# Trainium2 kernel of four conv layers: longer loops, loads on two queues, paired stores, and a bank of sums copied by two engines

## The reference

```python
# layer 0 runs on a group-normed x, layer 1 on x + layer 0
def _gn(v, G=8, eps=1e-5):          # mean and variance over 2 channels x 128 x 128
    ...
# layer 1: a global mean and max of the normed map, two gates from them
out1 = jnp.mean(x, axis=(2, 3), keepdims=True)
out3 = jnp.max(x, axis=(2, 3), keepdims=True)
wh_weight = jax.nn.sigmoid(jnp.tanh(conv1x1(conv1x1(x, Wc, bc) / (out1 + EPS), W2, b2)))
gray_weight = jax.nn.sigmoid(jnp.tanh(conv1x1(conv1x1(x, W1, b1) / (out3 + EPS), W3, b3)))
out = conv1x1(x * (1.0 + wh_weight + gray_weight), W4, b4)
# layer 2: rational functions of the 9 neighbours, summed
pw = wins[..., None] ** jnp.arange(DEG_P)                 # powers 0 to 5
P = jnp.einsum('pbchwi,fcpi->fpbchw', pw, A)
Q = 1.0 + jnp.abs(jnp.einsum('pbchwi,fcpi->fpbchw', pw[..., 1:5], Bc))
out = jnp.sum(P / Q, axis=(1, 3))
```

## Time and profile before

| | us |
|---|---|
| median of 3 runs | 9667.91 |
| lowest and highest run | 9665.2, 9704.05 |
| the profiled execution | 9659.51 |
| its span | 9657.6 |

### The profile page before, as it was taken

The page is one execution under the profiler, slowest core; times in us unless marked ns, Lnnn a source line. Parts: engine busy times, 40 slices in busy tenths (PEclk is TensorE's granted clock), DMA queues, the critical chain, the costliest instruction groups (busy, mean ns, idle before and its releaser), DMA issues. The chain is left out here.

```text
span 9657.6 us, 141494 instructions
## 1 busy us (share of the span) xinstructions
PE 8079.0 (84%) x35042; PEld 2745.1 (28%) x35042; DVE 7784.3 (81%) x9341; ACT 7530.9 (78%) x8315; POOL 6169.8 (64%) x3354
## 2 busy tenths in 40 slices
PE   5999999999999999402998999899899899992799
PEld 2333333333333333100222222222222222220233
DVE  6777777777777776775999999899899999894787
ACT  4666666666666666365999999999999999992887
POOL 3555555555555554002999999999999999992111
PEclk9999999999999999756999999999999999996899
DMA  2000000000000000254333233323332233235555
GB/s 87 12 13 11 12 11 11 11 11 11 13 11 11 12 11 3 110 170 134 70 71 68 59 68 71 69 61 65 71 71 64 60 70 71 65 64 134 132 146 124
DMA packets 258449, 565.42 MB, mean 59 GB/s; under 512 B 71659, under 2 KB 179787, under 8 KB 244183
## 3 DMA queue, kind: packets, MB, share of 16 engines
q1 hardware_dynamic: 221746, 536.51, 22.6%
q0 software_dynamic: 35744, 17.87, 1.0%
HBM read 367.15 MB, written 186.72 MB: 57 GB/s over the span
## 5 line engine op out<-in xcount | busy, mean ns | idle before, releaser
L1226 POOL TENSOR_TENSOR l_a<-l_a 128x1018 f32<-128x1018 f32 x2117 | 3919.7, 1883 | 334.9 <-ACT l_a L1401 327.7
L1356 DVE TENSOR_TENSOR l_r<-l_pps,l_a 128x509 f32<-128x509 f32 x4234 | 2653.6, 680 | 377.7 <-PE l_pps L1239 311.3
L1401 ACT ACTIVATE l_a<-l_a 128x2036 f32<-128x2036 f32 x1194 | 2269.4, 1901 | 52.6 <-ACT l_a L1394 46.8
L1239 PE MATMUL l_qps<-l_mv,wst 123*128 123x509 bf16 x4248 | 1283.8, 384 | 754.8 <-DMA l_mv<-pw 408.3
L1394 ACT ACTIVATE l_a<-l_qps 128x1018 f32<-128x1018 f32 x1593 | 1604.1, 1016 | 172.5 <-PE l_qps L1239 145.8
L599 POOL TENSOR_TENSOR a_pr<-a_pr 128x768 f32<-128x768 f32 x384 | 896.5, 2335 | 807.9 <-DVE a_pr L537 792.0
L1239 PE MATMUL l_pps<-l_mv,wst 123*128 123x509 bf16 x4234 | 1334.8, 381 | 56.5 <-DVE l_r L1356 46.0
L675 ACT ACTIVATE a_g<-a_fps 128x512 f32<-128x512 f32 x1152 | 645.4, 595 | 755.7 <-PE a_fps L419 631.8
L1292 PE MATMUL l_aux<-l_r,l_sums 128*32 128x509 f32 x8448 | 1140.7, 606 | 0.5 <-issue 0.4
L1362 DVE TENSOR_SCALAR l_a<-l_qps 128x1018 int32<-128x1018 int32 x796 | 961.3, 1208 | 9.3 <-PE l_qps L1239 8.0
L537 DVE TENSOR_TENSOR a_pr<-a_qkv,a_at 128x768 f32<-128x768 f32 x576 | 854.8, 1536 | 2.2
(11 more groups left out here) (180 smaller groups left out, 11911.9 us busy)
## 6 DMA issues: line engine op xcount, KB each, us to landing
l_mv<-pw SPq DMA_DIRECT2D x1608, 79.5 KB
l_gx<-g SPq DMA_DIRECT2D x66, 1040.0 KB
l_sh<-planes SPq DMA_DIRECT2D x536, 127.2 KB, 6.2
planes<-l_s SPq DMA_DIRECT2D x66, 1018.0 KB, 4.6
a_xt<-g SPq DMA_DIRECT2D x192, 160.0 KB, 3.3
pw<-pw_hi SPq DMA_DIRECT2D x20, 1000.0 KB
pw<-pw_mid SPq DMA_DIRECT2D x20, 1000.0 KB
pw<-pw_lo SPq DMA_DIRECT2D x20, 1000.0 KB
```

The costliest lines, as they stand in the source:

```text
L1226: g.tensor_tensor(a, a, a, ALU.mult).then_inc(sq_p, 1)
L1239: return t.matmul(out, wst[:, k, n * P:(n + 1) * P], x[:, n // NPP, cols], start=True, stop=True)
L1356: v.tensor_tensor(to, pps[:, (2 * m + h) % P_BANKS, 0:SUB], pair_of(A, m)[:, h, :], ALU.mult).then_inc(mul_done, 1)
L1401: s_.activation(a, a, ACT.Abs_reciprocal_sqrt, bias=1.0).then_inc(root_done, GROUP)
```

## The change

- **Loops.** Layer 0's loop body holds 20 chunks instead of 4 (3 rounds instead of 15). Layer 2's holds 18 supertiles instead of 6 (3 rounds), and the remaining 12 supertiles stand written out behind the loop. SP's own loop in layer 2 stays at 6.
- **norm0.** Quarters 0 and 2 are loaded and stored by SP, 1 and 3 by ScalarE's queue.
- **Layer 1, front.** X is loaded as two halves and the pieces of x1 in turn, by both queues. The addition walks rows: X in runs of 16 elements, G with a stride. Each piece gets a small maximum (`tops`), and the last reduction reads 1024 elements. GpSimd makes a block of ones, and SP stores it to DRAM.
- **Powers.** A slot holds two chunks, there are two slots, and SP stores a pair at a time: one DMA of 2 MB per part with rows of 1600 elements instead of 800. The weights follow pair 0.
- **Layer 2, start.** VectorE's three fills are gone. SP loads the three supertiles back to back and behind each one the ones from DRAM; TensorE waits for 5 DMAs (`c_in` 80) instead of 2.
- **Layer 2, sums.** The copies of subs 1 and 3 are VectorE's, those of subs 0 and 2 stay with ScalarE.
- **Layer 3, front.** All pieces of X come first on SP, the weights behind them; Y comes on ScalarE's queue with five slots. The weights are worked on at piece 6. Half of the stores are issued by each queue.

```diff
+ROUNDS = 20
...
-    with engine.Fori(0, (LEAD_OUT - LEAD_IN) // TURNS) as thrice:
-        for i in range(TURNS):
-            body(Plan(thrice * TURNS + (LEAD_IN + i), (LEAD_IN + i) % TURNS, LEAD_IN))
+    with engine.Fori(0, (LEAD_OUT - LEAD_IN) // ROUNDS) as again:
+        for i in range(ROUNDS):
+            body(Plan(again * ROUNDS + (LEAD_IN + i), (LEAD_IN + i) % TURNS, LEAD_IN))
...
+        def load(e, k):
+            e.dma_start(X[:, k * HW // 4:(k + 1) * HW // 4], x[:, k * HW // 4:(k + 1) * HW // 4]).then_inc(x_in[k], 16)
...
+                for k in (0, 2):
+                    load(sp, k)
...
+                for k in (1, 3):
+                    load(act, k)
                 norm.scalar_part(act)
+                for k in range(1, W // COLS, 2):
+                    store(act, k)
...
+            def load(e, half):
+                rows = slice(half * HW // 2, (half + 1) * HW // 2)
+                e.dma_start(X[:, rows], x[:, rows]).then_inc(x_in[0], 16)
+                for k in range(half, LOADS, 2):
+                    n = HW // LOADS
+                    e.dma_start(G[:, k * n:(k + 1) * n], x1[:, k * n:(k + 1) * n]).then_inc(x_in[k], 16)
...
-                    for k in range(LOADS):
-                        n = HW // LOADS
-                        if k == 0:
-                            sp.dma_start(X[:], x).then_inc(xb_in, 16)
-                            sp.dma_start(shift0[:], bias0).then_inc(xb_in, 16)
-                        sp.dma_start(G[:, k * n:(k + 1) * n], x1[:, k * n:(k + 1) * n]).then_inc(x_in[k], 16)
+                    sp.dma_start(shift0[:], bias0).then_inc(x_in[0], 16)
+                    load(sp, 0)
...
-                    image, laid = X[:].rearrange("p (h w) -> p w h", w=W), G.rearrange("p (w h) -> p w h", h=H)
+                    image, laid = X[:].rearrange("p (h w) -> p h w", w=W), G.rearrange("p (w h) -> p h w", h=H)
...
-                            e.wait_ge(x_in[j], 16)
-                            if j == 0:
-                                e.wait_ge(xb_in, 32)
-                            link(v.scalar_tensor_tensor(image[:, at, :], laid[:, at, :], shift0[:], image[:, at, :], ALU.add, ALU.add))
+                            e.wait_ge(x_in[j], 16 if j else 64)
+                            link(v.scalar_tensor_tensor(image[:, :, at], laid[:, :, at], shift0[:], image[:, :, at], ALU.add, ALU.add))
+                            v.tensor_reduce(tops[:, j, :], image[:, :, at], AX.X, ALU.max)
...
-                        at = k * n // H
-                        return image[:, at:at + n // H, :]
+                        j, part = divmod(k, norm.CHUNKS // LOADS)
+                        rows = n // cols
+                        return image[:, part * rows:(part + 1) * rows, j * cols:(j + 1) * cols]
...
-                    link(v.reduce_max(top[:, 0:1], X[:], AX.X))
+                    link(v.reduce_max(top[:, 0:1], tops[:].rearrange("p k h -> p (k h)"), AX.X))
...
-        hi = sb("pw_hi", [P, BUF, DEG, CH], BF16)
...
+        hi = sb("pw_hi", [P, SLOTS2, DEG, 2 * CH], BF16)
...
-                for k, (at, n) in enumerate(chunks):
+                for q in range(NPAIRS):
+                    at, n = chunks[2 * q][0], sum(n for _, n in chunks[2 * q:2 * q + 2])
+                    done = min(2 * q + 2, len(chunks))
...
-                        sp.wait_ge(ready, (k + 1) * DEG)
-                        sp.dma_start(lines[m, :, :, :, at:at + n], t[:, k % BUF, :, 0:n]).then_inc(stored[k % BUF], 16)
-                    if k == 1:
+                        sp.wait_ge(ready, done * DEG)
+                        sp.dma_start(lines[m, :, :, :, at:at + n], t[:, q % SLOTS2, :, 0:n]).then_inc(stored[q % SLOTS2], 16)
+                    if q == 0:
...
-                    if k >= BUF:
-                        dve.wait_ge(stored[k % BUF], k // BUF * STORES)
+                    if k // 2 >= SLOTS2:
+                        wait_stored(dve, k // 2 - SLOTS2)
...
-BODY = 6
+BODY, QUEUED = 18, 6
...
+COPY_DVE = {1, 3}
...
+    for s in range(LAG_LATE, LAG_LATE + NSUP % BODY * NSUB * NPAIR2):
+        step(NSUP // BODY, s)
...
                 for g in range(SLOTS):
-                    sp.wait_ge(mv_cleared, g + 1)
                     load_supertile(g, g)
+                    sp.dma_start(mv[KROWS - 3:KROWS, g].rearrange("p c n -> p (c n)"), ones).then_inc(c_in, 16)
+                    if g == 0:
+                        sp.dma_start(sums[:], l2w[0]).then_inc(c_in, 16)
+                        sp.dma_start(pick[:], l2w[1]).then_inc(c_in, 16)
...
-                with sp.Fori(0, NSUP // BODY - 1) as it:
-                    for u in range(BODY):
-                        g = it * BODY + u
+                with sp.Fori(0, NSUP // QUEUED - 1) as it:
+                    for u in range(QUEUED):
+                        g = it * QUEUED + u
...
-                pe.wait_ge(c_in, 32)
+                pe.wait_ge(c_in, 80)
...
-                for u in range(SLOTS):
-                    v.memset(mv[:, u], 1.0).then_inc(mv_cleared, 1)
...
+                    m = s - LAG_COPY
+                    sub, n = divmod(m, NPAIR2)
+                    u, j = divmod(sub, NSUB)
+                    if m >= 0 and n == 7 and j in COPY_DVE:
+                        dve.wait_ge(summed, it * (len(BURSTS) * SUBS) + len(BURSTS) * (sub + 2))
+                        v.tensor_copy(S[:, u % 2, j * SUB:(j + 1) * SUB], aux[:, 0:SUB]).then_inc(s_copied, 1)
...
-                    if m >= 0 and n == 7:
+                    if m >= 0 and n == 7 and j not in COPY_DVE:
...
+            YSLOTS = 5
...
+            def store(e, half):
+                for k in range(PIECES):
+                    e.wait_ge(g_ready, k + 1)
+                    lo = k * ROWS // CROWS
+                    hi = lo + ROWS // CROWS if k < PIECES - 1 else NCK
+                    for j in range(half * QUAD // 2, (half + 1) * QUAD // 2):
+                        to = g3[lo:hi, :, :, j, :].rearrange("k e c n -> (e c) k n")
+                        src = G[32 * j:32 * j + 32, lo * CROWS:hi * CROWS, :].rearrange("p (k r) w -> p k (r w)", r=CROWS)
+                        e.dma_start(to, src).then_inc(g_stored, 16)
...
                     for k in range(PIECES):
                         n = HW // PIECES
                         sp.dma_start(X[:, k * n:(k + 1) * n], x2[:, k * n:(k + 1) * n]).then_inc(x_in[k], 16)
-                        if k >= 3:
-                            sp.wait_ge(added, k - 2)
-                        at = PW + k * ROWS * PW
-                        rows = out2[:, LEAD:].rearrange("c (b n) -> b c n", b=NB)[:, :, at:at + ROWS * PW]
-                        sp.dma_start(Y[:, k % 3, :], rows).then_inc(x_in[k], 16)
...
+                    norm.sync_part(sp, pair)
+                    for t, src in ((sw, l3w[0]), (scaler, l3w[1]), (bw, l3w[2]), (place, l3w[3]), (cbias, l3w[4]),
+                                   (mask, l3w[5]), (pick, l3w[6])):
+                        sp.dma_start(t[:], src).then_inc(w_in, 16)
+                    store(sp, 0)
...
-                        if p == 3:
+                        if p == 6:
...
+                    for k in range(PIECES):
+                        if k >= YSLOTS:
+                            act.wait_ge(added, k - YSLOTS + 1)
+                        at = PW + k * ROWS * PW
+                        rows = out2[:, LEAD:].rearrange("c (b n) -> b c n", b=NB)[:, :, at:at + ROWS * PW]
+                        act.dma_start(Y[:, k % YSLOTS, :], rows).then_inc(x_in[k], 16)
                     norm.scalar_part(act)
+                    store(act, 1)
```

More of the change, by code:

```diff
@@ L156 @@
 LEAD_IN, LEAD_OUT = 3, NCHUNKS - 1
-assert FS == 64 and 2 * HREST == P and SETS * FS == P and (LEAD_OUT - LEAD_IN) % TURNS == 0
+assert FS == 64 and 2 * HREST == P and SETS * FS == P and ROUNDS % TURNS == 0 and (LEAD_OUT - LEAD_IN) % ROUNDS == 0
 class Plan:
@@ L207, in _ @@
             def _(sp):
-                for k in range(4):
-                    sp.dma_start(X[:, k * HW // 4:(k + 1) * HW // 4], x[:, k * HW // 4:(k + 1) * HW // 4]).then_inc(x_in[k], 16)
+                for k in (0, 2):
+                    load(sp, k)
                 norm.sync_part(sp, pair)
[L211 to L214, removed]
+                for k in range(0, W // COLS, 2):
+                    store(sp, k)
                 sp.wait_ge(edges, 2)
@@ L717, in _, with layer1 @@
                 steps(act, body)
-def layer1(nc, x, x1, bias0, x2, pair, w1, raw2, pieces, wst, pw):
+def layer1(nc, x, x1, bias0, x2, pair, w1, raw2, pieces, ones, wst, pw):
     TILE = 1024
@@ L747, in layer1 @@
             top = sb1("l1_top", [P, 8])
+            tops = sb1("l1_tops", [P, LOADS, H])
+            one = sb1("l1_one", [ONES, SUB], BF16)
             stat = sb1("l1_stat", [P, 8])
@@ L798, in _ @@
                         sp.dma_start(flat, part2[:, m, :]).then_inc(stored, 16)
+                    sp.wait_ge(one_made, 1)
```

(19 more changed lines are left out.)

76 lines of the change are left out of this document (31 added, 45 removed).

## The result

| | median (us) | lowest to highest |
|---|---|---|
| before | 9685.95 | 9665.2 to 9704.05 |
| after | 9529.2 | 9524.66 to 9541.86 |

The account below looks back on a forecast made before the run. ScalarE was taken to bound layer 2's steady state, 61.59 of 62.97 us per supertile; stores bound the powers. Terms -50 -51 -56 -25 +17 -16 +5 -18 make -194: 9474 us against the median, range 9415 to 9565.

Parts of the forecast that it names:

- Edges: Loop jumps back in layers 0 and 2: 12 and 8 fewer, at 4.2 and 6.2 us each, give -51 and -50 us.
- Copies: Layer 2: two of four copies of sums per supertile leave ScalarE, 0.85 us each supertile, -56 us over 66.
- The rival in which VectorE's copy holds back the ring: Layer 2: VectorE's copy delays TensorE and ScalarE, supertile stays at 62.97 us, copies give nothing, 9530 us; chance 0.15.
- Powers: Powers stage: paired stores with longer rows cut a chunk from 17.09 to 15.4 us, -34, first store +9.3; together -25.
- The line through two packet sizes: Powers' stores: packet prices of 74.1 and 627 ns put a 3200-byte row at 133 ns, against 148 for two of 1600.
- The late first store: Start of the powers' stores: the first store waits for hi of chunk 1, +9.3 us.
- Layer 1, front: VectorE's work at layer 1's start: statistics -10, addition -7, maximum +1; together -16 us.
- a cost named at norm0: norm0: quarters 0 and 1 on two queues share the engines and arrive together at about 12.9 us, +4.8, taken as +5.
- Start of layer 2: TensorE waits for DMAs behind all 72 loads, starting 42 us into the stage instead of 25: +17 us.
- Layer 3, front: Loads and stores on two queues at layer 3's start: -15 for loads, -3 for stores, together -18 us.
- the -15 of the loads: Layer 3's front: last piece added 96 us after the start instead of 111, -15 us.
- The base: Whole kernel: the sum is made against one profiled execution, 9659.5 us, 8.4 below the median of 9667.9.

## Why the prediction was right, and where its terms were off

**Edges: right.** -51 in layer 0, measured -51.5 by the stage and 46.2 by undoing it. -50 in layer 2: 102.5 less 55 of steady time is 47.5, undone 47.9. The price of a jump back, 4 and 6 us, was read from intervals alone, and it held when the number of jumps changed. In layer 2 two small errors cancel: the two edges left cost 4.7 instead of 6.2 each, 3 less, and the long body and the code behind the loop cost 5, where the forecast took 0. The Trainium skill, "Runtime: NRT & Kernel Launch", section "Instruction fetch mechanics", has a taken branch whose target isn't at hand wait for a fetch; the four edges left in after, each 3.7 to 4.7 us longer than a steady interval, with nothing above 0.3 between them, agree.

**Copies: right.** -56, measured -55 from the intervals, -51 by undoing it; each copy taken from ScalarE paid until two were gone. The rival in which VectorE's copy holds back the ring did not come at two copies. The third and fourth together gain nothing, which ScalarE's busy time alone would not say.

**Powers: too high.** The line through two packet sizes gave 133 ns for a row of 3200 bytes, and 129.8 was measured, but a pair took 31.3 us, 15.65 per chunk, where 15.4 was priced: -29 instead of -34. The late first store was priced right, +9. Together -20, and -14.5 was measured against -25. The remaining 5 are likely at the first pair and the weights behind it, where SP's issues of six of the weights took 18.8 us instead of 7.4; no run separated them.

**Layer 1, front: right in its work, wrong in its start.** Addition 3.67, maximum 2.29 and statistics 2.46 per piece make 8.3; with the last reduction the work is 16.7 shorter, as priced. But the first addition came 6.6 us later, a cost named at norm0 and not carried over: two queues bring the first pieces together and late, and with one queue it came 5.6 sooner again. That leaves -10 for -16.

**Start of layer 2: right in sign, too small.** The place was right, the ones behind 72 loads. The term that was mis-sized is the rate: 146 GB/s came from a window of 12 us, and here the queue moved 133 (4420:4465), so that the 72 loads needed until 52.5 instead of 42: +27.5 for +17.

**Layer 3, front: wrong.** The step that failed is the weights at piece 6, which were costed at nothing. They held VectorE for 12 us in after (16.6 between the last two additions, 5.0 with the weights last), and the -15 of the loads was 0 in this pair of profiles and +7 on average over all. The stores took 27.6 us (8746.07 to 8773.62) instead of 36.4, -9 instead of -3, and that holds in every profile: 27.2 to 28.0 with two queues, 36.2 to 36.7 with one. Together -9 in this pair and -1 on average, for -18.

Why two queues store faster stays open. By the Trainium skill, "DMA: Bandwidth & Descriptors", section "Issuing engines are not separate DMA queues", only issue time is saved, and SP did issue for 32.3 of the 36.4 us. But the DMA engines were busy for 89% of the time before (8897:8933) and 93% after (8746:8773.6) on the same 4736 packets, 108 and 87 ns each, so issue alone does not account for it. norm0 shows that two queues can also be paid for with a later first piece.

**The base, and luck.** The sum was made against a profile that had 724.2 in the rest of layer 3, while the kernel before has 752.8 in its second; the two medians happen to differ by just what the other stages give. The missing 37 are the powers (10), layer 2 (11, its start above all), layer 1's start (5), layer 3's front (9) and small ends. Every stage that was off gained less than forecast; the time is inside the range since the three large terms, the edges of two layers and the copies, came within 3 us each.

Three sums in the recorded text are slightly off and change nothing. 13.7 MB at 150 GB/s are 91 us, not 93; Y is 8.45 MB by its queue's row in after, not 8.26; and 28 us of issues with 2 to land are 30, not 32.

## What to carry to other kernels

Where a loop's jump back stalls all engines, read the price from the intervals between equal instructions: the stretch that holds no edge against the mean of all. Put what is waited for first ahead of bulk loads in a queue, and give the first piece the whole bandwidth instead of sharing it with the second. Before a term is measured against one profile, look whether a stage with the same code has the same length in another: here two stages did not, by 38 and 12 us. Work that is moved to a later place is not free there because it was hidden at the earlier one.

## What the runs showed of the hardware

- Packets of 1600 and 3200 bytes took 74 and 130 ns, and norm0's large ones of about 16.6 kB 627 ns, an estimate from their mean rate. Twice the row brought 9% more bytes per second, with the DMA engines 53% and 51% busy.
- The same 32 stores of layer 3 took 36.2 to 36.7 us from one queue and 27.2 to 28.0 from two.
- Walking X in runs of 16 elements instead of columns took the addition from 4.69 to 3.67 us and the statistics of 4 x 512 elements from 3.75 to 2.46, the value of a contiguous read in layer 3.
- With a single round of 60 chunks a chunk of layer 0 took 57.07 us, with three rounds of 20 or fifteen of 4 it took 57.52, beyond the edges.
- Straight code behind a loop ran 0.2 us per supertile (0.3%) slower than inside it.
